# A loop over six turns on every engine, written out as six copies with constant waits

## The reference

```python
x = x + L0_attn(layernorm(x))   # softmax over queries, only its diagonal is kept, times V
x = x + L0_ffn(layernorm(x))    # 2 layers: 8-head attention in windows of 64 with
                                # rotary factors and l2-normalised q and k, then a GELU MLP
x = x + L1_attn(layernorm(x))   # 16 heads of 8 dims, causal softmax, output projection
x = x + L1_ffn(layernorm(x))    # 8 experts of width 256, two chosen per token, and a shared one
```

## Time and profile before

| | |
|---|---|
| median of 3 runs | 1997.63 us (1995.62 to 1999.28) |
| the profiled execution | 1997.42 us, of which the span from first to last instruction is 1995.6 us |
| busy share of the span | PE 82%, DVE 57%, ACT 49%, POOL 30% |
| mean granted clock of TensorE | 0.914 of full |
| instructions recorded | 32820 |
| transfers of instructions | queue q8 105 packets, 1.72 MB; queue q14 76 packets, 0.62 MB |

### The profile page before, as it was taken

The page is one execution under the profiler, slowest core; times in us unless marked ns, Lnnn a source line. Parts: engine busy times, 40 slices in busy tenths (PEclk is TensorE's granted clock), DMA queues, the critical chain, the costliest instruction groups (busy, mean ns, idle before and its releaser), DMA issues.

```text
span 1995.6 us, 32820 instructions
## 1 busy us (share of the span) xinstructions
PE 1638.1 (82%) x11632; PEld 956.7 (48%) x11632; DVE 1146.3 (57%) x2565; ACT 986.9 (49%) x2277; POOL 605.0 (30%) x396
## 2 busy tenths in 40 slices
PE   2666569899699978999699978999688988998579
PEld 1334235555446444464546544454445555455235
DVE  6543357557484576557494566646574585744614
ACT  1435253844547544754447535664538445662042
POOL 2624071605242061613324051512515051510000
PEclk9787679999899998999799998999899998999689
DMA  4010011011300122001410123001310123002201
GB/s 131 19 24 1 0 44 41 21 38 44 86 21 2 46 57 65 21 30 32 93 29 5 38 65 64 22 22 32 85 30 21 38 60 68 22 17 61 64 2 53
DMA packets 37333, 80.57 MB, mean 40 GB/s; under 512 B 6782, under 2 KB 22654, under 8 KB 33776
## 3 DMA queue, kind: packets, MB, share of 16 engines
q1 hardware_dynamic: 37152, 78.22, 15.6%
HBM read 54.74 MB, written 8.78 MB: 32 GB/s over the span
## 4 chain that ended last, share of the span: by engine, by line
PE 54%; DVE 16%; ACT 15%; issue 9%; POOL 5%; DMA 1%; DVEq 0%; SPq 0%; POOLq 0%; ACTq 0%
PE ps L350 47%; ACT work L766 8%; PE ps L355 6%; DVE cmax L1116 4%; ACT big L846 4%; POOL small L1237 2%; DVE small L1004 1%; DVE fxn L917 1%; POOL frs L1237 1%; POOL work L1262 1%; DVE x L1198 1%; DVE work L972 1%; POOL work L1273 1%; DVE fst L904 1%; DVE work L971 1%
## 5 line engine op out<-in xcount | busy, mean ns | idle before, releaser
L1262 POOL TENSOR_TENSOR work<-work 128x1024 f32<-128x1024 f32 x64 | 151.0, 2359 | 462.1 <-DVE work L972 461.6
L350 PE MATMUL ps<-bxt,mw 128*128 128x512 f32 x576 | 278.2, 605 | 8.2 <-DVE big L1210 8.2
L350 PE MATMUL ps<-maskb,identb 128*128 128x128 bf16 (+1 forms) x1152 | 237.1, 249 | 47.2 <-ACT work L766 28.2
L766 ACT ACTIVATE work<-ps,pbias,small 128x128 f32<-128x128 f32 x512 | 228.8, 528 | 53.5 <-DVE pbias L1008 53.1
L355 PE MATMUL ps<-ident,work 128*128 128x128 f32 x1056 | 175.2, 313 | 62.7 <-ACT work L766 40.2
L1116 DVE TENSOR_REDUCE cmax<-ps 128x1 f32<-128x384 f32 (+3 forms) x352 | 199.5, 631 | 24.8 <-PE ps L350 24.6
L1237 POOL TENSOR_TENSOR small<-small,consts 128x8 f32<-128x8 f32 x128 | 208.2, 1640 | 5.0 <-DVE small L981 5.0
L350 PE MATMUL ps<-wqkv,h 128*128 128x512 f32 x384 | 188.1, 623 | 23.7 <-ACT v L726 12.0
L1293 POOL TENSOR_TENSOR work<-work,prec 128x1024 f32<-128x1024 f32 x64 | 134.3, 2099 | 209.9 <-DVE prec L999 209.9
L846 ACT ACTIVATE big<-ps 128x512 f32<-128x512 f32 x320 | 167.7, 638 | 58.1 <-PE ps L350 57.8
L868 ACT ACTIVATE big<-ps 128x512 f32<-128x512 f32 x144 | 85.2, 596 | 210.3 <-PE ps L350 209.4
(11 more groups left out here) (163 smaller groups left out, 2600.9 us busy)
## 6 DMA issues: line engine op xcount, KB each, us to landing
mw<-in_experts SPq DMA_DIRECT2D x72, 384.0 KB, 3.1
pk<-scr_parts SPq DMA_DIRECT2D x48, 192.0 KB
pq<-scr_parts SPq DMA_DIRECT2D x144, 64.0 KB
v<-v SPq DMA_DIRECT2D x16, 512.0 KB, 4.5
v<-v SPq DMA_DIRECT2D x16, 384.0 KB, 6.2
scr_parts<-big SPq DMA_DIRECT2D x8, 768.0 KB, 3.7
xin<-in_x SPq DMA_DIRECT2D x8, 256.0 KB, 3.4
out<-x SPq DMA_DIRECT2D x8, 256.0 KB, 6.0
```

What stands on the lines that cost most here:

```text
L350: return nc.tensor.matmul(o, a, b, start=start, stop=stop, skip_group_check=True)
L766: i = nc.scalar.activation(pr[:, m, a, p, :], fb[2 * (m % 2) + a][:, p * P:(p + 1) * P], ACT.Exp, bias=pbias[:, m, k:k + 1], scale=rn[:, m ...
L1262: nc.gpsimd.tensor_tensor(qk[:, m, :], qk[:, m, :], part[m % 2], ALU.add).then_inc(l_add.sem, 1)
```

## The change

The loop statement is replaced by a Python loop, so the six turns are recorded one behind the other. The steps, their order in a turn, the tiles and the transfers stay. `t` is now a number, so all waits are for constants, and no engine has the instructions that count, compute or jump.

```diff
     for half in (enter(0), leave(0), enter(1)):
         for _ in half:
             pass
-    with engine.Fori(0, SEQS - 2) as t:
+    for t in range(SEQS - 2):
         merge(chain(leave(t + 1), enter(t + 2)), back(t))
     merge(leave(SEQS - 1), back(SEQS - 2))
     for _ in back(SEQS - 1, last=True):
```

## The result

The written-out kernel takes 1965.19 us (1962.75 to 1965.94, 4 runs) against 1996.78 us before; the ratio is 0.984, with a 95% interval of 0.9824 to 0.9856. That is 31.6 us less. The forecast was 1964.2 us, in a range of 1954 to 1978.

A forecast was written before the change was run, and what follows sets the result against it. PE, busy 82% of the span, was taken to bound the kernel loosely. Five turns at 4.57 + 1.7 us give 31.4, registers 1.8: 33.2 off 1997.4 makes 1964.2 us, range 1954 to 1978.

The forecast's parts named there:

- The jump back: At the ends of turns 0 to 4: five taken jumps go, each worth 4.57 us as read at L1035.
- all engines stand at once: At each jump back: nothing covers its 4.57 us, and DVE, PE and ACT then start together.
- The comparison with the tail: Turn 4 against the tail, entered without a jump: four places behind L1195 come 4.57, 6.25, 8.00 and 8.30 us sooner.
- The clock's half: Two mid-turn stretches at granted clock 0.50, 1.68 and 1.75 us: half expected to go, 1.7 us a turn.
- all gone: Rival: both slow stretches vanish in every jumped turn, saving 41.8 us, time 1955.6 us; chance 0.2.
- all kept: Rival: only the jump goes, slow stretches stay, saving 24.7 us, time 1972.7 us; or less, 1977.4; chance 0.22.
- The registers: At the gates, L1182 to L1210: register instructions cost 0.30 us a turn in six turns, 1.8 us; elsewhere nothing.
- 1.5 + 31.4: Turns 1 to 5: registers at 0.30 us a turn, plus 31.4 us for five turns' jumps and clock.
- The rule that speaks against it: At the jumps: compare-and-branch takes about 108 ns, so five cost 0.5 us and time stays at 1997 us.
- the standing was not the jump's: Rival at turn ends: the wait has an unseen cause and stays; 1997 us less 1.8; chance 0.03.
- straight supply falls behind: Rival over the written-out program: packets hold PE up; 4.5 us at one in five gives 2059 us; chance 0.02.
- What I said of "issue": Sign in the chain that ended last: "issue" share falls by about 22 us of the span, 1 point.

The follow-up runs named there:

- e1: Kernel before with six loops of one pass each in place of the loop, registers kept, no jumps back: 1964.87 us, ratio 0.984.
- e3: Kernel before with two turns in each loop pass, so two jumps back in place of five: 1975.8 us, ratio 0.9892.
- e4: Written-out kernel with an empty loop of two passes at each turn's end on every engine: 1966.62 us, ratio 0.9853.
- e2: Kernel before with its loop kept and a hint at the head of each pass naming the jump's target: 1964.54 us, ratio 0.9836.
- e7: Kernel before with PE and DVE written out, the loop kept on ACT, POOL and SP: 1965.76 us, ratio 0.9838.
- e10: Kernel before, loop, registers and jumps kept, with extra and doubled matmuls added to hold the clock up: 1972.84 us, ratio 0.988.
- e9: Written-out kernel with extra constant matmuls where PE waits and the first matmul of 16 scores doubled: 1933.37 us, ratio 0.9681.
- e11: Kernel before with the loop's jump target hinted, plus extra and doubled matmuls to hold the clock up: 1947.44 us, ratio 0.9749.
- e5: Kernel before with the loop kept on PE alone, the other engines written out: 1999.2 us, ratio 1.0004.
- e6: Kernel before with the loop kept on DVE alone, the other engines written out: 1998.82 us, ratio 1.0013.

## Why the prediction was right

*The jump back.* Right in kind and near in size. e1 shows that the jumps are the whole of the gain, e3 that it goes with their number, e4 that a near jump is free, and e2 that the standing is a wait for the target's instructions. The term was 4.57 us a turn, from the tail at L1035. That "all engines stand at once" was too wide: POOL shows no idle time from it, and ACT's stop lies beside waiting (e7). The stops also differ more than the one end of a turn that was read: in before DVE stands 4.46 to 6.93 us behind the jump, not only 4.79. With the clock held up otherwise a jump costs 5.9 us (e10 against e9), since it also brings one slow stretch. That 4.57 was less has to do with the clock in the first 35 us. Here is that stretch of turn 4 of before, then of turns 3 and 4 of after:

```profile
1183.50:1218.50 35.00, 22.08 (x249) 16.15 (x248) 16.32 (x35) 20.91 (x74) 12.78 (x8) 0.71 0.41 94
```

```profile
941.50:976.50 35.00, 25.68 (x314) 18.92 (x315) 16.04 (x35) 20.77 (x75) 12.79 (x8) 0.76 0.50 115
1161.80:1196.80 35.00, 24.35 (x317) 17.53 (x318) 16.47 (x35) 20.76 (x75) 12.79 (x8) 0.85 0.48 112
```

The tail of before has 0.76 as turn 3, and against these two the jump costs 4.6 to 4.7 us at L1035. Against turn 4 of after, at 0.85, it is 44.26 - 38.39 = 5.9.

*The comparison with the tail* carried the forecast. The same four places in after, as distances from L1195, which answer to the earlier trace rows:

| place | turn 4 of before | tail of before | turn 3 of after | turn 4 of after |
|---|---|---|---|---|
| L1035 | 44.26 | 39.69 | 39.54 | 38.39 |
| L1262, POOL | 74.44 | 68.19 | 68.04 | 68.57 |
| second `brs` | 134.68 | 126.68 | 126.52 | 128.61 |
| L1068 | 174.97 | 166.67 | 166.51 | 168.61 |

The last two columns come from these rows of the timelines of after, for turn 4 (its L1195 at 1161.80):

```profile
1200.19 0.69 DVE L1035 TENSOR_TENSOR work<-h,ps 128x512 f32<-128x512 f32 x1 [1.22 <-PE ps L350]
...
1230.37 2.36 POOL L1262 TENSOR_TENSOR work<-work 128x1024 f32<-128x1024 f32 x1 [44.36 <-DVE work L972]
...
1290.41 0.20 POOL L1237 TENSOR_TENSOR brs<-bmv,consts 128x4 f32<-128x4 f32 x1 [5.13 <-DVE bmv L911]
...
1330.41 0.69 DVE L1068 TENSOR_TENSOR x<-ps,x 128x512 f32<-128x512 f32 x1 [0.34 <-PE ps L355]
```

Turn 3 of after is the tail of before to 0.2 us at all four places. Turn 4 is a turn with the two slow stretches: 1.2 us ahead at L1035, 2.1 behind at L1068.

*The clock's half.* Expected were slow stretches at half of the ten places; they stand at four of ten, and at three of five new ones at 190 us, of which the turns of before had one (turn 1). The two rivals beside the forecast, all gone and all kept, describe turns 2, 3, 5 and turns 1, 4; neither describes the kernel. Not foreseen was that the tail, once it stands behind other turns, would have them too, which gave 2 us back.

*The registers.* The term was 0.30 us a turn and 1.8 together; e1 puts it at 0.1 to 0.3 a turn and shows no difference in the kernel's time. The time came out within 1 us in part by luck: turns 1 to 5 gave 34.4 where 1.5 + 31.4 was written and turn 0 gave 1.5 in place of 0.3, while the tail took back 2.3 where nothing was written. That the turns' part is near is no luck. Turn 3 of after, without the stretches, is 8.4 us shorter than a turn of before was on average, where 4.57 + 3.43 + 0.30 = 8.3 was read from the tail, and the stretches that stayed cost 1.5 us a turn on average, where 1.7 was written.

*The rule that speaks against it.* By e4 a near branch takes 53 ns on DVE and 142 ns on PE in the median, and by the earlier trace rows PE's branch over a whole turn 5224. The Trainium skill gives about 108 ns for a compare-and-branch ("Advanced Engine Details and Errata", Control Flow Timing); that is the size of the near ones, and misses the far one by nearly fifty times. The Trainium skill's other rule ("Runtime: NRT & Kernel Launch", Instruction fetch mechanics), that a jump out of the blocks held waits for its target, is the one that the traces bear out: 5.48 us at a turn's end with the jump, 0.80 with its target named (e2).

*The other rivals.* That the standing was not the jump's is excluded by e2. That straight supply falls behind is excluded for the written-out kernel: fewer packets than before and no stops. In the kernels with a loop and extra matmuls (e10, e11) PE may have met it, for 2 to 3.6 us at a time.

*What I said of "issue"* was that its share would fall by about 1 point of the span. It fell from 9% to 4%, but e1 keeps 9% at the same time as after. Most of that share was register work that held nothing up; 5% of the span, read as time to be won, would have promised 100 us.

## What to carry to other kernels

Look at a loop's edge on each engine apart: how long its first operation stands behind its last one with "issue" as the reason, against the same place where the loop is left. If that is microseconds, name the jump's target ahead or write the turns out; both gave all of the gain here, and doing it on one of several critical engines gave none. Then look at the granted clock: pauses of TensorE cost again behind them, and cheap matmuls in those pauses gained another 32 us. Trace such a kernel again: where PE has less slack, stops appeared that no trace had shown before.

## What the runs showed of the hardware

- Behind a jump back over a turn's code an engine stands with "issue" as the reason for 3 to 7 us (ACT 2.9 to 3.4, PE 2.8 to 6.5, DVE 4.2 to 6.9 over before, e3, e5, e6, e7 and e10; PE's branch itself takes up to 7.8 us where PE alone loops). A jump back to the instruction just before takes at most 63 ns on DVE and 357 ns on PE, and no standing follows.
- A hint at the head of the body brings PE's branch from 5224 to 370 ns in the median, and the whole loop to the time of straight code.
- Turns settle in patterns: with identical instructions they take 220.3, 221.8 or 223.4 us in one execution, and the difference is where TensorE is granted 0.50.
- With the granted clock held at 1.00 for whole turns, the same work and 48 extra matmuls take 216.9 us. Over the kernel, holding it up in PE's pauses gained as much as taking the five jumps out, 31.8 and 31.6 us.
- With hinted loop and extra matmuls PE stood 1.97 and 3.61 us in straight code (e11), with loop and jumps 2.07 (e10), each time with an instruction packet landing within the stop.
